# A two-layer attention and expert kernel: attention's sixteen sequences written out in line on every engine, and K loaded by the SP queue in place of GpSimd's

## What is computed

```
qkv    = layernorm(x) @ W_attn.T            # 512 x 384 for a sequence
scores = q @ k.T / sqrt(8) + slope * (pos_k - pos_q), -inf where pos_k > pos_q
y      = softmax(scores) @ v                # 16 heads of 8 channels
x      = x + y @ W_proj.T
```

## Time and profile before

| | |
|---|---|
| median of 3 runs | 1710.12 us (1705.8 to 1710.37) |
| profiled execution | 1709.79 us |
| its span, first to last instruction | 1707.7 us |
| mean granted TensorE clock | 0.829 |
| busy in the span | PE 1230.7, DVE 1187.3, ACT 850.4, POOL 991.2 us |
| attention | from the start to about 680 us |

### The profile page before, as it was taken

One profiled execution on the slowest core, in us unless ns is written; L12 is line 12 of the kernel. 1 busy time (PEld: TensorE's weight loads), 2 busy tenths in 40 slices (PEclk: granted clock), 3 DMA queues, 4 the chain that ended last, 5 costly groups with the idle time before them and its releaser, 6 DMA issues. The chain is left out here.

```text
span 1707.7 us, 35056 instructions
## 1 busy us (share of the span) xinstructions
PE 1230.7 (72%) x9528; PEld 723.2 (42%) x9531; DVE 1187.3 (70%) x3304; ACT 850.4 (50%) x2073; POOL 991.2 (58%) x1023
## 2 busy tenths in 40 slices
PE   2888788888688888492155466526199999999997
PEld 1333343333233333482044233226056555555555
DVE  2888787878587875485722599867866666666664
ACT  1577676677576777012112466534144444444443
POOL 1455565555455552340045389864278888888887
PEclk7899999999899998555567556555599999999999
DMA  4533343433233341460033201200423333333333
GB/s 103 153 82 92 83 110 89 100 89 90 70 91 86 82 105 50 155 211 29 0 92 70 67 25 42 102 7 37 171 39 42 41 41 42 42 41 43 42 41 41
DMA packets 88430, 125.49 MB, mean 73 GB/s; under 512 B 22434, under 2 KB 59106, under 8 KB 84242
## 3 DMA queue, kind: packets, MB, share of 16 engines
q0 software_dynamic: 41120, 45.22, 17.1%
q1 hardware_dynamic: 39170, 65.85, 11.8%
q10 hardware_dynamic: 8032, 12.93, 2.1%
HBM read 65.72 MB, written 57.68 MB: 72 GB/s over the span
## 5 line engine op out<-in xcount | busy, mean ns | idle before, releaser
L551 DVE TENSOR_REDUCE mx<-psS 128x2 f32<-128x768 f32 (+3 forms) x384 | 387.8, 1041 | 132.5 <-PE psS L442 131.2
L622 ACT ACTIVATE probs<-psE 128x512 f32<-128x512 f32 (+2 forms) x768 | 351.7, 523 | 133.4 <-PE psE L456 130.0
L344 POOL TENSOR_SCALAR_AFFINE_SELECT probs<-probs 128x512 f32<-128x512 f32 x256 | 161.6, 642 | 262.7 <-ACT probs L622 262.5
L2036 POOL DMA_INDIRECT out<-ex_y,ex_idx x144 | 236.8, 1645 | 47.1 <-issue 42.7
L456 PE MATMUL psE<-qop,kop 63*128 63x512 bf16 (+3 forms) x1024 | 187.3, 311 | 56.6 <-ACT probs L622 28.8
L2027 POOL DMA_INDIRECT ex_xg<-expert_tab,ex_idx x144 | 142.0, 986 | 66.0 <-issue 41.7
L468 PE MATMUL psY<-probs,vaug 128*32 128x512 f32 (+3 forms) x2048 | 169.8, 450 | 10.3 <-POOL probs L344 10.3
L2010 DVE SCALAR_TENSOR_TENSOR ex_h<-ex_psG,ex_w,ex_up 128x352 f32<-128x352 f32 x144 | 84.1, 584 | 109.2 <-ACT ex_w L2111 104.7
L442 PE MATMUL psS<-kop,qop 61*128 61x128 bf16 (+3 forms) x1024 | 142.1, 310 | 0.0
L2094 PE MATMUL ex_psY<-ah_w3s,ex_hT 128*128 (+1 forms) x864 | 133.3, 290 | 0.8 <-ACT ex_hT L2105 0.7
L437 PE MATMUL psS<-maskq,spread 64*128 64x128 bf16 (+2 forms) x1536 | 116.0, 227 | 13.3 <-DVE mx L551 13.1
(11 more groups left out here) (317 smaller groups left out, 2564.1 us busy)
## 6 DMA issues: line engine op xcount, KB each, us to landing
y_scr<-ysb SPq DMA_DIRECT2D x64, 256.0 KB, 2.7
qkv_scr<-parts SPq DMA_DIRECT2D x32, 384.0 KB, 2.6
qop<-qkv_scr POOLq DMA_DIRECT2D x30, 192.0 KB, 4.8
kop<-qkv_scr POOLq DMA_DIRECT2D x30, 192.0 KB, 6.4
expert_tab<-table_rows SPq DMA_DIRECT2D x1, 4352.0 KB, 13.5
pj_num<-y_scr SPq DMA_DIRECT2D x16, 256.0 KB
pj_rec<-rec_scr SPq DMA_DIRECT2D x16, 256.0 KB
x_scr<-x_all ACTq DMA_DIRECT2D x16, 256.0 KB, 3.3
```

What stands on the lines that cost most here:

```text
L344: pool.affine_select(diag, diag, [[0, HG], [1, P]], ALU.is_ge, 0.0, base=0, channel_multiplier=-1).then_inc(s_msk, 1)
L551: dve.tensor_reduce(out, src, AX, ALU.max).then_inc(s_su, 1)
L622: act.activation(probs[st % 2][j][:, 2 * p + h0:2 * p + h0 + nh, :].rearrange("p h q -> p (h q)"), ring_bank(st, k)[:, 0:nh * W[j]], ACT.E ...
L2036: pool.indirect_dma_start(out, bass.IndirectOffsetOnAxis(ap=idx[t % 8][:], axis=0), y[m][:], None, compute_op=ALU.add).then_inc(s_sc[m], 16)
```

## The change

All sixteen sequences are written in line on the four engines that had the loop. The K loads of sequences 1 to 15 move from GpSimd to SP, behind SP's y write of step 2, and count on `s_first`; Q's stay with GpSimd on `s_op`. The waits of `split_rest` and of TensorE follow: six DMAs for each sequence on either semaphore.

```diff
             def body(n, b, last):
                 for st in range(G):
                     step(n, b, st, last)
-            for b in range(2):
-                body(b, b, False)
-            with eng.Fori(1, nb // 2 - 1) as i:
-                for n in range(2):
-                    body(n, 2 * i + n, False)
-            for b in (nb - 2, nb - 1):
+            for b in range(nb):
                 body(b % 2, b, b == nb - 1)
...
                     sp.dma_start(y_scr[bass.ds(bb, 1), HG * g:HG * g + HG].rearrange("b h r q -> (b h r) q"), ysb[g % 2][:])\
                         .then_inc(s_yw[g % 2], 16)
+                if st == 2 and not last:
+                    sp.wait_ge(s_pw[1], 16 * b + 16)
+                    if isinstance(b, int) and b == 0:
+                        sp.wait_ge(s_rows, 128)
+                    for p in range(2):
+                        place_k(sp, 1 - n, s_first, p)
...
                 pool.wait_ge(s_rst, 4 * b + 2 * s + 2)
-                if b == 2:
-                    pool.wait_ge(s_first, 96 + 16 * 12)
-                if b > 2:
-                    pool.wait_ge(s_op, 16 * 12 * (b - 2))
+                if b == 2 or b > 2 and s == 1:
+                    pool.wait_ge(s_first, 96 + 16 * (12 + 6 * (b - 2)))
+                elif b > 2:
+                    pool.wait_ge(s_op, 16 * 6 * (b - 2))
...
                         clear_future(u, j)
-                        if st == 2 and more and j < 2:
-                            if j == 0:
-                                pool.wait_ge(s_pw[1], 16 * b + 16)
-                            place_k(pool, 1 - b % 2, s_op, j)
...
                     if st == 0 and there(G * b):
-                        if isinstance(b, int) and b == 0:
-                            pe.wait_ge(s_first, 96 + 16 * 12)
-                        else:
-                            pe.wait_ge(s_op, 16 * 12 * b)
+                        pe.wait_ge(s_first, 96 + 16 * (12 + 6 * b))
+                        if not isinstance(b, int) or b:
+                            pe.wait_ge(s_op, 16 * 6 * b)
                         pe.wait_ge(s_rows, 128)
```

## The result

The changed kernel takes 1751.22 us (median), the kernel before 1707.96 in the same runs: ratio 1.0266, 95% interval 1.0227 to 1.0306. It is 43 us slower. The profiled execution has a span of 1748.3 us against 1707.7.

A forecast was written before the change was run, and what follows sets the result against it. Attention was taken as a ring of three engines, none full, its time a count of steps. Fourteen sequences at 41.8 us instead of 39.56 add 31.4, the last load 5.1: +36 on 1709.79 gives 1746 us, range 1703 to 1778.

The forecast's parts named there:

- Straight code and the stop of GpSimd (1, 2): In attention, loop branches, register work and GpSimd's one stop in sequence 10 go: 31.8 us less, 10.3 of it the stop.
- K's landing (3): K from SP lands 21.3 us after step 2's transposes (M2), on few DMA engines; step 0's transposes come 3.6 us later.
- Rival A: K from SP lands no later than from GpSimd and stays hidden: 1678 to 1664 us, chance 0.14.
- The half clock: After waiting for K, TensorE runs at 1.2 GHz at each sequence's start: +0.7 us before step 0's mark (M0), +0.2 after.
- The last load: From step 2 of sequence 14 to step 0 of sequence 15: 23.4 us, not 18.27, so +5.1 us.
- The max rows (4): Step 3's wait for max rows, 1.60 to 1.90 us a sequence, should shrink or go; hidden while K ends later.
- The sum: Over attention, 14 x (41.8 - 39.56) = +31.4 us and +5.1 for the last load, together +36 us.

The follow-up runs named there:

- the eight-row kernel: The changed kernel with SP's K loads of sequences 1 to 15 cut into twelve DMAs of eight different rows, no broadcast source: 1675.97 us, ratio 0.9820.
- the one cut load: The changed kernel with one of SP's six K loads, the 16-row one of the second half, cut into two of eight rows: 1714.12 us, ratio 1.0051.
- the last two kernels: Q's second half issued by SP, its first half by GpSimd in 4 KB rows, then in 8 KB rows: 1652.24 and 1658.70 us, 0.9685 and 0.9719 of the kernel before.

## Why the prediction was right

It named 1746 us and a range of 1703 to 1778; 1751.22 was measured. By its steps:

**Straight code and the stop of GpSimd (1, 2).** Predicted: 31.8 us, of which 10.3 for the stop and so 21.5 for the code. The straight code alone gave 21 us with the stop still in it, and none of the kernels with 90 DMAs or fewer from GpSimd in attention shows the stop. In the straight kernel the stopped sequence takes 8.7 us more than the mean of the others, so 10.3 was somewhat too much. The taking of 37.29 us for an undisturbed sequence was right within 0.2: 37.5 in the eight-row kernel.

**K's landing (3).** Predicted M2 + 21.3, measured 21.40. It came from one row of the kernel's start, less 1.1 us for Q's head start. The engines were read rightly from the shares 0.19 and 0.13; the packet counts bear them out, and the eight-row kernel and the one cut load show that they are the cause. But the way to 21.3 was partly luck: it counts from K's first issue, and the kernel with K ahead of y shows that an issue 1.37 us sooner brings 0.2. What sets the landing is the work of the busiest engines, not the moment of issue. The Trainium skill's rule for the number of engines (DMA: Bandwidth & Descriptors, Why a DMA increments its semaphore by 16 and not by 1) agrees with these traces, for a broadcast source too (390 and 1050 packets, shares of 0.12 and 0.53). Rival A fails, and with it what it leaned on, that page's section Issuing engines are not separate DMA queues, by which another issuer changes only its own time: here K landed at M2 + 21.4 from SP and 16.0 from GpSimd. What A named, 1664 to 1678 us, is what the eight-row kernel takes, 1676.

**The half clock.** Predicted +0.7 before M0 and +0.2 behind it. Measured: transposes to M0 1.95 us, M0 to M1 10.75 in the mean, against 1.43 and 10.00 at full clock, so 1.3 us and not 0.9. This term was sized 0.4 us a sequence too small, 5 us in all, and makes 42.2 of 41.8. It was taken from one branch gap of 2.43 us, and I read the gaps in the earlier trace rows as all alike. They are not: behind three of the five the clock was at half, behind the other two, 2.58 and 2.63 us long, it stayed full:

```profile
271.84 0.65 PE L380 MATMUL psE<-ident,xn 128*128 128x128 f32 x4 [2.63 <-issue]
```

In the changed kernel all 14 waits, 2.6 to 4.4 us long, have the half clock beside them, and five of them, 3.6 to 4.4 us long, for twice as long as the others. The end has more of it, which I left out. The window in which sequence 15 begins:

```profile
671.00:684.50 13.50, 12.81 (x102) 5.24 (x102) 6.89 (x8) 6.81 (x14) 2.54 (x4) 0.50 0.29 89
```

From M0 of sequence 15 on, attention takes 3.5 us more than before.

**The last load.** Predicted 23.4 from M2 of 14 to M0 of 15, measured 22.8.

**The max rows (4).** This step failed. I wrote that with K behind it on its own queue the wait should shrink or go. It did not: 7.6 us from issue to landing and not 7.8, waits of 21.6 us in total against 23.7. K was never what held it: it is 7.6 to 7.8 us in all nine kernels in which Q came from GpSimd in six DMAs of 8 KB rows, with K on SP, on GpSimd or on both. The kernels with Q in 4 KB rows and with half of Q on SP show that it is Q's packets from GpSimd. The error cost nothing here, since K ended later, but it hid the gain that the last two kernels found.

**The sum.** Sequences 0 to 14 gave +37.0 where +31.4 was named, the last load +4.6 for +5.1, the end +3.5 for nothing: +45 and not +36 for attention. Later parts of this profiled execution were some 5 us shorter than in the one before, which no step of the change touches. That the time came out within 5 us of 1746 is in part luck; the mechanism, K's landing on few engines, is not.

## What to carry to other kernels

Before a load is moved to another queue, ask how many DMA engines each queue spreads it over: a broadcast outermost dimension of 3, 2 or 1 puts SP's load on three, two or eight engines, and the tail at a DMA share of 2/16 shows it. Cut such a load into DMAs with enough different rows (75 us here). A small transfer that someone waits for should not share its engines with large packets of another queue: put the large ones behind it in its own queue, or make them smaller.

## What was not expected of the hardware

- GpSimd stops once at its 129th DMA, in four kernels, at 454, 438, 604 and 427 us, for 6.3 to 10.9 us, whichever load it is and whatever its bytes. The traces show when it ends: the last of the 128 DMAs before it lands at 463.38, 446.11, 608.14 and 431.90, and GpSimd goes on 1.80 or 1.81 us after that in each, in the last two while SP's transfers still run (a DMA share of 0.40 and 0.53 just before). So the stop lasts until its own DMAs have landed, and 1.8 us more. In the kernels where the 129th falls among the indirect DMAs of the last part, with little under way, no such stop is seen; why it comes at 129, no run shows.
- A transfer of 8 KB of max rows takes 1.72 us alone and 7.6 us beside six loads of 8 KB rows from the other queue.
- An issue 1.37 us sooner brought 0.2 us at landing.
